# A fused attention and expert kernel on one core: the scatters of finished rows one tick later in the sweep, the last batch's weights two ticks earlier

## The reference

```python
x = x + xattn(layernorm(x), ctx, mask)      # softmax(x c' / sqrt(512)) c, 64 batches of 128 x 128
h = layernorm(x)
scores = softmax(h @ G)                     # 8 experts
w = top_2(scores)                           # the weights of the two best, 0 for the others
gated = silu(h @ gate_w[e].T) * (h @ up_w[e].T)
x = x + sum_e w[e] * (gated @ down_w[e].T + (h @ lora_A[e].T) @ lora_B[e])
```

## Time and profile before

| | us |
|---|---|
| three runs | 517.6, 517.89, 519.47 |
| median | 517.89 |
| the profiled execution | 517.89 |
| its span in the profile | 515.8 |
| PE busy | 494.1 (96%) |
| DVE busy | 444.9 (86%) |
| ACT busy | 369.8 (72%) |
| POOL busy | 293.6 (57%) |

### The profile page before, as it was taken

The page is one execution under the profiler, slowest core; times in us unless marked ns, Lnnn a source line. Parts: engine busy times, 40 slices in busy tenths (PEclk is TensorE's granted clock), DMA queues, the critical chain, the costliest instruction groups (busy, mean ns, idle before and its releaser), DMA issues.

```text
span 515.8 us, 16239 instructions
## 1 busy us (share of the span) xinstructions
PE 494.1 (96%) x4040; PEld 434.1 (84%) x4040; DVE 444.9 (86%) x1758; ACT 369.8 (72%) x1012; POOL 293.6 (57%) x423
## 2 busy tenths in 40 slices
PE   8999999999999999798999999999999999999984
PEld 7888888888887888696887999889999999999973
DVE  5899999999999997796788899899888888888865
ACT  4778878878877788786777777677566666666642
POOL 4237767777668777745775444444544445454444
PEclk9999999999999999999999999999999999999998
DMA  8999999999999999999998999979999999999822
GB/s 320 397 304 362 408 410 398 407 401 404 405 405 375 408 328 303 395 365 410 406 354 312 389 383 368 326 276 390 417 412 415 416 417 417 415 414 413 332 105 83
DMA packets 65607, 189.10 MB, mean 367 GB/s; under 512 B 9582, under 2 KB 9710, under 8 KB 65520
## 3 DMA queue, kind: packets, MB, share of 16 engines
q1 hardware_dynamic: 44352, 120.20, 61.5%
q0 software_dynamic: 20800, 67.65, 33.1%
q10 hardware_dynamic: 368, 0.22, 0.2%
HBM read 114.04 MB, written 78.73 MB: 374 GB/s over the span
## 4 chain that ended last, share of the span: by engine, by line
PE 60%; DVE 7%; issue 5%; POOL 4%; DMA 2%; ACT 1%; another core or an unknown queue 1%; POOLq 0%; DVEq 0%; SPq 0%; ACTq 0%
PE rd L528 13%; PE bank L528 12%; PE bank L470 11%; PE rd L546 7%; PE rd L547 6%; PE rd L535 3%; PE bank L372 2%; DMA x_sb<-in_x 2%; DVE xe L816 2%; PE rd L412 1%; PE rd L413 1%; PE bank L351 1%; POOL x_rows L1207 1%; POOL out_x L1222 1%; DVE stats L739 1%
## 5 line engine op out<-in xcount | busy, mean ns | idle before, releaser
L654 ACT COPY hT<-bank 128x512 f32<-128x512 f32 x140 | 81.8, 584 | 30.2 <-PE bank L470 16.3
L1207 POOL DMA_INDIRECT x_rows<-xe x64 | 64.9, 1014 | 42.7 <-issue 22.5
L528 PE MATMUL rd<-wg_sb,hT 128*128 x560 | 80.6, 287 | 2.1 <-ACT hT L654 1.6
L528 PE MATMUL bank<-wg_sb,hT 128*128 x560 | 80.3, 286 | 0.0
L372 PE MATMUL bank<-cc_sb,xnT 128*128 128x136 f32 x512 | 80.1, 286 | 0.0
L528 PEld LDWEIGHTS rd<-wg_sb,hT 128*128 128x128 f32 x560 | 72.6, 190 | 3.1 <-issue 3.0
L528 PEld LDWEIGHTS bank<-wg_sb,hT 128*128 128x128 f32 x560 | 72.6, 190 | 0.3 <-issue 0.2
L546 PE MATMUL rd<-dn_a,ggT_a 128*128 x140 | 67.0, 479 | 1.9 <-DVE ggT_b L1098 1.0
L372 PEld LDWEIGHTS bank<-cc_sb,xnT 128*128 128x128 f32 x512 | 68.4, 191 | 0.2
L1222 POOL DMA_INDIRECT out_x<-z_shared x41 | 39.9, 972 | 40.2 <-issue 35.0
L1108 DVE SCALAR_TENSOR_TENSOR z_shared<-rd,z_shared 128x512 f32<-128x512 f32 x77 | 57.7, 749 | 1.9 <-PE rd L547 0.2
(11 more groups left out here) (186 smaller groups left out, 1196.1 us busy)
## 6 DMA issues: line engine op xcount, KB each, us to landing
cc_sb<-in_cc SPq DMA_DIRECT2D x64, 532.0 KB
z_shared<-z_rows SPq DMA_DIRECT2D x41, 516.0 KB
x_sb<-in_x SPq DMA_DIRECT2D x64, 256.0 KB
z_own<-z_rows SPq DMA_DIRECT2D x29, 516.0 KB
z_shared<-x_rows SPq DMA_DIRECT2D x36, 260.0 KB
z_own<-x_rows SPq DMA_DIRECT2D x34, 260.0 KB
z_rows<-pad SPq DMA_DIRECT2D x8, 516.0 KB
wg_sb<-in_wg SPq DMA_DIRECT2D x8, 288.0 KB
```

Of the source, the lines that this page charges most:

```text
L528: mm = pe.matmul(gu_ps[q % 2][:, 0:GU], hT[:, q % 2, k, :], wg_flat[:, bass.ds(at + k * GU, GU)], start=(k == 0), stop=(k == KD - 1))
L654: act.copy(hT[:, q % 2, :, :], hT_ps[q % 2][:].rearrange("p (k s) -> p k s", k=KD)).then_inc(hT_ready, 1)
L1207: pool.indirect_dma_start(out=x1_rows[:, :], out_offset=rows_at(row, ROW1), in_=row, in_offset=None, bounds_check=ROWS - 1, oob_is_err=Fal ...
```

## The change

The scatter in the sweep is that of tile `t-10` instead of `t-9`, its wait for `x1_ready` being the same; what is left over behind the sweep is then four tiles instead of three. The exponential of the last batch goes from tick 6 to tick 4, its weights from tick 7 to tick 5. The four last scatters stand behind blocks 2, 5, 8 and 11.

```diff
-RANKED, SHARED, WEIGHED, COUNTED, SUMMED, TABLE, OVERLAP, SKIP = 2, 5, 7, 7, 21, 25, 26, 30
+RANKED, SHARED, COUNTED, SUMMED, TABLE, OVERLAP, SKIP = 2, 5, 7, 21, 25, 26, 30
...
-                if t == WEIGHED - 1:
+                if t == SHARED - 1:
                     router_exp(NB - 1)
...
-                if t == WEIGHED:
+                if t == SHARED:
                     weigh_sum(NB - 1)
                     number(NB - 1)
                     weigh_inverse(NB - 1)
...
-                if in_sweep(t, 9):
+                if in_sweep(t, 10):
 
                     pool.wait_ge(x1_ready, min(t - 2, B))
-                    scatter_x1(t - 9)
+                    scatter_x1(t - 10)
...
-            for n in range(SWEEP - 9, B - TB):
+            for n in range(SWEEP - 10, B - TB):
                 scatter_x1(n)
...
                 scatter_block(q)
-                if q % 3 == 2 and q // 3 - 1 in range(TB):
-                    scatter_x1(B - TB + q // 3 - 1)
+                if q % 3 == 2 and q // 3 in range(TB):
+                    scatter_x1(B - TB + q // 3)
```

## The result

| | before | after |
|---|---|---|
| median of four runs | 517.78 us | 526.17 us (525.43 to 526.51) |
| ratio | | 1.0152, 95% interval 1.0129 to 1.0176 |
| the profiled execution | 517.89 us | 524.49 us |
| its span | 515.8 us | 522.4 us |

The account below looks back on a forecast made before the run. DVE was taken to pace the sweep and PE the blocks. Parts 1, 2, 3, 5 and 6 gave 0 and part 4 -0.1 us, so 517.8 us against 517.89, no change that can be told; range 515.9 to 519.8 us.

Parts of the forecast that it names:

- Part 1: Sweep scatter one tick later: POOL's waits for L889 nearly vanish, but DVE sets the pace; gain 0, bound 1.0 us.
- Part 2: End of the sweep: six scatters in a row instead of five, hidden by gaps; cost 0, or 0.3 us without cover.
- Part 3: Last batch's exponential on ACT, tick 6 to 4: no wait, 1.6 us in hand; value 0, bounds -0.22 and +0.22.
- Part 4: Four weight instructions on DVE, tick 7 to 5: new place covered; value -0.1 us, bounds -0.51 and +0.51.
- Part 5: Last four scatters three blocks earlier: POOL catches up in later idle time; value 0.
- Part 6: DVE copies L1097 lengthened or freed by the four moved scatters: value 0, with ±1.1 us.
- The early scatter makes that stall grow: Slower rival: scatter near 225.5 us lengthens ACT's stall ahead of L695 at 236.51; 520.8 us, chance 0.10.
- The sign of being wrong that I gave: If time moves by over 2 us, it shows in L695's starts, a stall gone, halved or grown, not in the sweep.

Follow-up runs that it names:

- e5: The changed kernel, unaltered, run again beside the kernel before on a chip without late counts: 506.42 us, ratio 0.9992.
- e14: The changed kernel with a power of 128 x 1 on POOL behind each scatter of tiles from 50 on and of the first 48 blocks: 529.10 us (1.0197).
- e9: The changed kernel with one wait more, block 1's tanh L695 waiting for POOL's L1176 behind the row of six scatters: 524.04 us (1.0131).
- e13: The kernel of e9 again (changed kernel, block 1's tanh waiting for L1176), in another set: 523.34 us (1.0117).
- e12: The kernel before with the sweep's scatter one tick later alone, on a chip with late counts: 523.22 us (1.0100).
- e2: The kernel before with the earlier exponential, weights and four last scatters, the sweep as it was: 507.37 us (1.0011).
- e15: The kernel before with two more scatters, of 8 numbers a row, behind its row of four at the end of the sweep: 522.52 us (1.0078).
- e16: The sweep's part on the kernel before, powers behind scatters of tiles 50 to 59, exponential, weights and last four scatters later: 521.08 us (1.0017).
- e18: The kernel before with powers behind scatters of tiles 50 to 59 and blocks 0 to 9, exponential, weights and last four scatters later: 513.49 us (0.994).
- e17: The kernel before with powers behind scatters of tiles 50 to 59, exponential, weights and last four scatters later: 520.65 us (1.0022).

## Why the prediction was wrong

**Part 1** was right on DVE, which is 0.24 us late after 62 ticks. POOL's waits for L889 in the sweep are gone, but other waits took their place: L816 now holds the scatters up for 22.7 us in 13 waits, where it had been 2.0 in 2. It failed at the end of the sweep: the row of three over 197.61 to 201.18 us holds TensorE's counts, and L816 of tick 62 comes 2.03 us later. The prediction looked for who waits for POOL, found L1166 and no one else, and set the term at 0. It measured about 2 us.

**Part 2 is the step that failed most.** It set one scatter more in the row at cost 0: 1.28 us of POOL, all but 0.3 us of it in a gap, and the rest hidden ahead of block 0's scatter. On POOL that was right: on the chip of e5 the last L1175 stands at 215.71, where I had said 216.0. (In after it stands at 218.19.) But the row itself was taken for harmless to everyone who doesn't wait for it. It is not, on such a chip: 6.48 - 2.03 = some 4.4 us more by block 1's tanh, of which 2.3 us are made up at block 2, where before stands. Why one scatter more weighs so much can be read in the rows. In before the row proper starts at 210.87, since its first scatter stands alone ahead of a gap, and the tanh of block 1 at 213.07 still slips through; the row of four ends at 215.67 and holds block 2. In after the sweep is 2 us late and the row reaches to 218.18, so it holds block 1 already, 2.5 us longer. The clock adds to it: behind the idle stretch the eight matmuls take 2.13 us instead of 1.24, and the tanhs of the blocks 3 and 4 come 2.99 and 2.39 us after the one before, 1.4 us over two ticks of 2.00. With it the loss is back at 5.67 us by block 4. The prediction had said that nothing is lost by the clock, from stretches in which TensorE was busy throughout.

**Part 3**: the exponential stands at 218.58 in e5, after 0.55 us of idle, where I had said 220.4 and none: ACT was there earlier than in the trace of before, whose late counts had slowed it. I had 1.6 us in hand in that trace and took it for a property of the kernel. Where POOL is made later the cover is gone, as in e14 (4.44 us). **Part 4** can't be seen by itself in after. **Part 5**, the four last scatters three blocks earlier, had value 0, and that failed too: the scatter of tile 60 behind that of block 2 stands in the row of four from 230.08 to 235.15 us, and block 7's tanh comes behind it, at 235.93. The loss goes there from 5.62 to 8.58 us. e9 and e13, which hold the whole change, have the same tick of 4.92 and 4.72 us; e12, with the sweep's part alone, has 2.32. Block 10's tanh, 5.06 us after the one before in after, is not new: it is the one of the earlier trace rows, with 5.01 in before. What block 7 loses is for the most part made up by block 35 (5.98 us), where before had late tanhs of its own. So parts 3 to 5 hold up to a third of the loss, by 1.0100 against 1.0152 on different chips, and how much exactly stays open. On a chip without late counts they are e2: 1.0011 (0.9991 to 1.0032), which bears out 0.

**Part 6**: the copies L1097 of after take 220, 221 and 519 ns, nearly as in the earlier trace rows. The rule that was weighed there, of the Trainium skill (SBUF — State Buffer, section Who interferes with whom), would have had copies of up to about 1 us, as an estimate; the longest of any run takes 0.66 us (e9).

**The rivals.** The one that ended slower, "The early scatter makes that stall grow", had the sign right, and that the early scatter would show in the starts of L695. It had the mechanism and the place wrong: that stall (1.70 us of idle in the earlier trace rows, 5.01 between the starts) stayed as it was with 5.06, and the early scatter made a new one at block 7, by making a row of four. I wrote "the engine named, PE, is not late otherwise, and I find no cause in the rows", and gave the rival a price from that one stall. The cause stood one engine over: POOL's four close scatters from 230.64 us. Had I set the stalls of ACT beside POOL's rows, I would have asked what a row of six does. The sign of being wrong that I gave, a stall in the starts of L695 and none in the sweep, was half right: 2.03 us are in the sweep.

**What stays open.** Why some chips show it and others don't: nothing in the program differs. By what way POOL's scatters hold TensorE's counts, and only those. Whether the recording of the trace has a part in it: the chips with late counts are those whose traces lack a quarter of TensorE's records, and each run on record has a span and a clock, so none shows the time without recording. That rival is untested. And whether the lateness alone, made by hand where there is none, makes the whole loss: e9 and e13 were meant for that and fell on the other kind of chip. (In e14 ACT stood for 4.44 us with no count late, the clock fell behind it, and the kernel was slow; but it had other waits too.) That close rows are the cause is shown by e15 (longer row of nearly no bytes: later counts, +0.78%) and by e14, e16 and e18 (gaps: no count over 0.44 us late in their place). That they are all of the loss is argued, from the places where it arises.

## What to carry to other kernels

Where an engine is idle and the one it waits for was done long ago, by its own row, set the other engines' rows beside the gap before you call it unexplained: the cause may be one that nobody in the program waits for. Count how many indirect transfers a change puts one right behind the other, and, where chips show late counts, keep some 0.8 us between all of them by other work of the same engine, if that engine has the time; otherwise the gaps become a wait of their own. And a stall in the trace of before is not a property of the kernel alone: time the kernel on a second chip before you build on it.

## What the runs showed of the hardware

- On five of eight chips, and on that of the result, TensorE's recorded semaphore counts come late while POOL issues indirect transfers 0.30 to 0.46 us apart: by up to 6.2 us with six in a row (e15; 3.8 in after), 3.4 with four (before), 1.4 with two that stand alone (after), and they are let go 0.5 to 1.6 us behind the row, if no scatter follows (in e16 one followed 1.24 us behind a row of five, and they were let go 2.7 us behind it). Lone scatters have counts late by up to 0.5 us. Rows with gaps of 0.8 us and more throughout had 0.43 us in e14, 0.42 in e16 and 0.44 in e18, and once 0.83 in e17. On the three other chips no count was late by over 0.07 us, and the kernel before takes 507 to 508 us instead of 517 to 519.
- The traces of the first kind of chip have 72 to 76% of TensorE's counts on record, those of the second all of them.
- An indirect scatter of 128 rows takes POOL 0.96 to 1.07 us and the next one starts 0.30 us later, for 8 numbers a row as for 520. A memset of 128 x 1 fits into the 0.30; four of them make it 0.36; a power of 128 x 1 makes it 0.80 us or a little more.
- POOL's wait for its own memset ahead of a scatter costs 0.80 us.
- TensorE's granted clock was at 0.67 on the mean from 220 to 225 us in after, behind 5 us in which it was busy for 2.68, and at 1.00 in before, behind 5 us with 3.29 us busy, and in e18, which had 5.00.
